# Attention in a one-core transformer kernel: 128-key score matmuls against four groups of 32 keys, with scores one step further ahead and the squares dealt out anew

## What is computed

```python
def _L0_attn_ref(x, w_qkv, w_proj, b_proj):      # x: (4, 1024, 256), H = 16 heads of 16
    qkv = jnp.einsum('btc,fc->btf', x, w_qkv)
    ...
    scores = jnp.einsum('bhqd,bhkd->bhqk', q, k) * hs ** (-0.5)
    p = jax.nn.softplus(scores)
    p = p * p
    p = p * jnp.tril(jnp.ones((t, t), dtype=p.dtype))
    attn = p / (jnp.sum(p, axis=-1, keepdims=True) + 1e-09)
    out = jnp.einsum('bhqk,bhkd->bhqd', attn, v)
```

## Time and profile before

| what | value |
|---|---|
| median of three runs | 1603.25 us (1602.64 to 1603.25) |
| the profiled execution | 1605.87 us |
| its span in the trace | 1604.0 us |
| attention phase in it | from 275.7 us to about 626 us |
| TensorE busy over the span | 1520.9 us (95%) |
| VectorE, ScalarE, GpSimd busy | 1216.4, 873.0, 411.4 us |
| DMA in the attention phase | about 100 GB/s |

### The profile page before, as it was taken

How to read it: one execution, slowest core, us unless ns; L and a number is a source line. 1 busy time by engine, 2 the same in 40 slices (tenths; PEclk the granted TensorE clock), 3 DMA queues, 4 the chain that set the end, 5 groups by cost and what they waited for, 6 DMA issues and landing times. The chain is left out here.

```text
span 1604.0 us, 28965 instructions
## 1 busy us (share of the span) xinstructions
PE 1520.9 (95%) x11188; PEld 1125.0 (70%) x11188; DVE 1216.4 (76%) x2334; ACT 873.0 (54%) x1372; POOL 411.4 (26%) x382
## 2 busy tenths in 40 slices
PE   8999898999999998999989999979999999899998
PEld 7888776444444446888867778756777777678777
DVE  4554797898999986664578888768777777688886
ACT  3333387988888886332332222278888887321220
POOL 0002111222122224100433221113555555211111
PEclk9999999999999999999999999999999999999999
DMA  4000065777777750000100000022333333100000
GB/s 159 26 1 14 20 188 178 100 95 106 106 101 102 100 72 2 14 1 1 40 27 8 1 1 1 1 69 78 102 101 107 106 107 107 40 14 27 14 27 27
DMA packets 57160, 95.83 MB, mean 60 GB/s; under 512 B 7904, under 2 KB 29632, under 8 KB 57024
## 3 DMA queue, kind: packets, MB, share of 16 engines
q1 hardware_dynamic: 56064, 93.38, 26.4%
q10 hardware_dynamic: 960, 0.59, 0.1%
HBM read 76.91 MB, written 17.04 MB: 59 GB/s over the span
## 5 line engine op out<-in xcount | busy, mean ns | idle before, releaser
L1438 DVE TENSOR_TENSOR att_weights<-att_weights 128x1024 f32<-128x1024 f32 (+1 forms) x224 | 267.7, 1241 | 39.4 <-ACT att_weights L1411 39.1
L928 DVE SCALAR_TENSOR_TENSOR X<-ps,moe_gsel,X 128x256 f32<-128x256 f32 x512 | 246.1, 483 | 63.5 <-PE ps L48 41.1
L1411 ACT ACTIVATE att_weights<-ps 128x1024 f32<-128x1024 f32 (+1 forms) x288 | 264.9, 992 | 39.8 <-PE ps L1347 20.5
L48 PE MATMUL ps<-w_experts_hi,moe_xh 128*128 128x512 f32 x512 | 205.1, 401 | 1.1 <-DVE X L928 1.1
L48 PE MATMUL ps<-w_experts_hi,moe_xl 128*128 128x512 f32 x512 | 203.3, 397 | 0.0
L48 PE MATMUL ps<-w_experts_lo,moe_xh 128*128 128x512 f32 x512 | 201.6, 394 | 0.0
L1367 PE MATMUL ps<-att_weights,att_v_ones 64*32 64x64 f32 (+5 forms) x2048 | 157.6, 400 | 0.0
L424 ACT ACTIVATE ffn_gates<-ps,ffn_gate_bias 128x512 f32<-128x512 f32 x72 | 49.5, 688 | 148.3 <-PE ps L48 126.6
L48 PEld LDWEIGHTS ps<-w_experts_hi,moe_xh 128*128 128x128 f32 x512 | 96.2, 188 | 27.9 <-DVE X L928 4.5
L48 PEld LDWEIGHTS ps<-w_experts_lo,moe_xh 128*128 128x128 f32 x512 | 96.1, 188 | 22.1
L48 PEld LDWEIGHTS ps<-w_experts_hi,moe_xl 128*128 128x128 f32 x512 | 96.3, 188 | 20.3
(11 more groups left out here) (281 smaller groups left out, 3672.1 us busy)
## 6 DMA issues: line engine op xcount, KB each, us to landing
ssm_lb<-decays SPq DMA_DIRECT2D x32, 512.0 KB, 4.7
ssm_rise<-decays SPq DMA_DIRECT2D x28, 512.0 KB, 3.9
qk_parts<-qkv_part SPq DMA_DIRECT2D x32, 384.0 KB, 2.8
q_stack<-qk_parts SPq DMA_DIRECT2D x64, 128.0 KB, 4.6
k_stack<-qk_parts SPq DMA_DIRECT2D x64, 128.0 KB, 7.8
att_q_stack<-qk_parts SPq DMA_DIRECT2D x64, 128.0 KB, 4.8
att_k_stack<-qk_parts SPq DMA_DIRECT2D x64, 128.0 KB, 8.8
out<-X SPq DMA_DIRECT2D x7, 512.0 KB, 2.9
```

The source lines that it names most:

```text
L48: ins = pe.matmul(out, l(k), r(k), start=first and n == 0, stop=last and n == len(passes) - 1)
L928: dve.scalar_tensor_tensor(out=x, in0=ring[:, e // 2, (e % 2) * C:(e % 2 + 1) * C], scalar=gsel[:, s, j, e:e + 1], in1=x, op0=ALU.mult, op ...
L1411: act.activation(Wt[:, u % WU, 0:n], scores(u)[:, 0:n], ACT.Softplus).then_inc(p_done, 1)
L1438: dve.tensor_tensor(wt, wt, wt, ALU.mult).then_inc(sq_done["dve"], 1)
```

## The change

The scores are computed by four matmuls with 32 keys each in place of one with 128 (`KG = 32`), each in its own column group; the masks too, and only for the groups that hold a masked key (two of four); the opening matmuls of UPPER units likewise become four over 128 rows. The matmul with zeros (L1358) goes, and the first REST tile opens the sum. The scores run five steps ahead of the values instead of four, and three of the four output stages stand one unit later. ScalarE squares the units 2, 7, 11 and 15 of a pass (before 6, 9 and 14), GpSimd none (before 11), VectorE 14 as before. What is computed stays the same.

```diff
--- before.py
+++ after.py
@@ -1278,11 +1278,12 @@
     step_units = [[u for u in range(NU) if step_of[u] == m] for m in range(NS)]
     BLOCK_STEPS = [m for m in range(NS) if m % PS == PS - 1 or pass_steps[m % PS + 1][0] != pass_steps[m % PS][0]]
     BLOCK_UNITS = [step_end[m] for m in BLOCK_STEPS]
-    STEPS_AHEAD = 4
-    TURN_LAG, COPY_LAG, DEN_LAG, OUT_LAG = 2, 7, 9, 10
+    STEPS_AHEAD = 5
+    TURN_LAG, COPY_LAG, DEN_LAG, OUT_LAG = 2, 8, 10, 11
     SU, WU = 3, 12
+    KG = 32
     assert NU % SU == 0 and NU % WU == 0
-    BY_ACT, BY_POOL = (6, 9, 14), (11,)
+    BY_ACT, BY_POOL = (2, 7, 11, 15), ()
     squarer = ["act" if u % PU in BY_ACT else "pool" if u % PU in BY_POOL else "dve" for u in range(NU)]
 
     def squares(by, i, u):
@@ -1333,18 +1334,21 @@
                 upper = segments[0][-1] == UPPER
                 pe.wait_ge(p_done, i * NU + u + 1)
                 if upper:
-                    low = slice(0, HALF)
                     pe.sem_inc(scores_free, 1)
-                    for r in range(2):
-                        pe.matmul(scores(u)[r * HALF:(r + 1) * HALF, 0].rearrange("p (s q) -> p s q", q=HALF), neg[low, low],
-                                  ident16[low, low].unsqueeze(1).broadcast_to([HALF, BANK // HALF, HALF]), start=True, stop=False)
+                    for g in range(P // KG):
+                        at = g * KG % HALF
+                        pe.matmul(scores(u)[g * KG:(g + 1) * KG, 0].rearrange("p (s q) -> p s q", q=HALF), neg[:, at:at + KG],
+                                  ident16[:, 0:HALF].unsqueeze(1).broadcast_to([P, BANK // HALF, HALF]), start=True, stop=False)
                 for n, (h, kj, t, c, q, w, part) in enumerate(segments):
-                    rows = slice(h % 2 * HALF, (h % 2 + 1) * HALF) if part == UPPER else slice(0, P)
-                    keys = slice(kj * P, kj * P + (HALF if part == UPPER else P))
-                    ins = pe.matmul(scores(u)[rows, t, c:c + w], SK[s][:, h, keys], SQ[s][:, h, q:q + w],
-                                    start=not upper, stop=n >= len(segments) - 2 if upper else part == FULL)
+                    groups = range(h % 2 * HALF, (h % 2 + 1) * HALF, KG) if part == UPPER else range(0, P, KG)
+                    for g in groups:
+                        keys = kj * P + (g % HALF if part == UPPER else g)
+                        masked = part == REST and g >= HALF
+                        ins = pe.matmul(scores(u)[g:g + KG, t, c:c + w], SK[s][:, h, keys:keys + KG], SQ[s][:, h, q:q + w],
+                                        start=not upper, stop=n >= len(segments) - 2 if upper else not masked)
                     if part == REST:
-                        ins = pe.matmul(scores(u)[:, t, c:c + HALF], neg[:, :], ident16[:, HALF:P], start=False, stop=True)
+                        for g in range(HALF, P, KG):
+                            ins = pe.matmul(scores(u)[g:g + KG, t, c:c + HALF], neg[:, g:g + KG], ident16[:, HALF:P], start=False, stop=True)
                 ins.then_inc(s_done, 1)
 
             def value_step(i, m):
@@ -1354,8 +1358,6 @@
                     pe.wait_ge(v_copied, 2 * (2 * i + s + 1))
                 if products[0][1] == 0 and not upper:
                     pe.wait_ge(o_done, (i * 2 + s) * BLOCKS + qb + 1)
-                    if qb == 0:
-                        pe.matmul(O(qb), ident16[:, :], neg[:, 0:1].broadcast_to([P, BANK]), start=True, stop=False)
                 for u in step_units[m]:
                     pe.wait_ge(sq_done[squarer[u]], squares(squarer[u], i, u))
                 if upper:
@@ -1365,7 +1367,7 @@
                     rows = slice(h % 2 * HALF, (h % 2 + 1) * HALF) if part == UPPER else slice(0, P)
                     values = va_up[rows, s, kj, h // 2] if part == UPPER and h % 2 else va[rows, s, kj, h]
                     ins = pe.matmul(O(qb)[h * 2 * HD:(h + 1) * 2 * HD, q0:q0 + w], values,
-                                    Wt[rows, (s * PU + unit) % WU, t, c:c + w], start=kj == 0 and part == FULL, stop=part == UPPER and kj == (qb + 1) * GT - 1)
+                                    Wt[rows, (s * PU + unit) % WU, t, c:c + w], start=kj == 0 and part != UPPER, stop=part == UPPER and kj == (qb + 1) * GT - 1)
                 ins.then_inc(pv_done, 1)
 
             def turn_output(n, i, k):
```

## The result

The changed kernel takes 1621.95 us in the median of 4 runs (1615.6 to 1628.21), the kernel before beside it 1602.95 us (1600.72 to 1603.25). The ratio is 1.0111, 95% interval 1.0086 to 1.0136: slower by 1.1%, 19 us, where 49 were forecast. The direction and the mechanism came as predicted; the forecast change is two and a half times too large, and the predicted 1652 us is wrong.

What follows compares the result with a forecast made beforehand. TensorE was taken to bound the attention's 21.3 us pass; afterwards 18.6 us of work, 5.3 idling for instructions and 0.5 slow clock make 24.4, 3.1 us x 16 = +49 us, so 1652 us in the median, range 1585 to 1700.

Steps and rivals of the forecast that it cites:

- What bounds the kernel before: Attention passes: TensorE is the bound, 20.5 us of work in a pass of 21.33, some 0.8 left for waiting.
- TensorE's own work after: Attention pass after the change: TensorE's steps sum to 18.6 us, with FULL scores 3.52, REST 4.48 and values 6.88.
- rival 4: Score steps: column groups overlap only twofold, +0.9 us on each of 8 large steps, pass 26 us, 1680 us; chance 0.03.
- rival 2: TensorE's score steps: changes of form stay or small weight loads replace them, pass near 20.5 us, 1590 us; chance 0.09.
- The number of packets: TensorE's instruction queue in the attention phase: 63 or so packets instead of 37, 3.9 a pass.
- Where the pauses lie: TensorE's issue idling: inside the stack loads, one or two pieces a pass, at distances of multiples of 256 instructions.
- How long they are: TensorE's idling for instruction packets queued behind stack loads: 5.3 us of every pass, from 2.7 to 7.9.
- the 640 instructions: TensorE's stock ten us into the loads: half a packet, one loaded and one more, lasting 13.2 us.
- The clock: TensorE's clock drops behind long gaps, worth up to 1.7 us of work; 0.5 us a pass taken.
- the forecast's own balance: Attention pass: 18.6 us plus idling equals the old 21.3 at 2.7 us of idling; below that, the change gains.
- rival 1: TensorE's instructions keep up with the column groups: a pass takes 19.4 us, median 1572 us; chance 0.18.
- Rival 3: TensorE's idling at its upper bound, 7.9 us, clock down after each: pass 27 to 28 us, about 1700; chance 0.10.

Runs made afterwards that it cites:

- groups_only_paced: Changed kernel with the steps ahead, lags and squares of the kernel before, its stack loads issued one at a time: 1585.55 us, ratio 0.9881.
- squares_only: Kernel before with only the new squares, four in a pass on ScalarE and none on GpSimd: 1607.25 us, ratio 1.0019.
- after_paced: Changed kernel with its 16 stack loads of a pass issued one by one along the next pass: 1580.51 us, ratio 0.9865.
- half_loads: Changed kernel without the key stacks' reloads in passes 3 to 16, query stacks still loaded at once: 1578.16 us, ratio 0.9834.
- after_noload: Changed kernel with the stack reloads of passes 3 to 16 left out: 1578.30 us, ratio 0.9849.
- paced_mix: Changed kernel with loads one at a time and unit 11's square given from ScalarE back to GpSimd: 1583.22 us, ratio 0.9864.

## Why the prediction was right and wrong

- **What bounds the kernel before**: right in the main. TensorE, with a pass of 21.27 us where 21.33 was read: less work on TensorE alone makes it 20.36 (groups_only_paced). But TensorE is not alone, as squares_only shows: a fourth square on ScalarE, which the forecast had well below the bound at 19.2 us, made the pass 21.86.
- **TensorE's own work after**: too low by 0.4 us. In a pass without pauses of after_paced, from start to start, FULL scores before values take 0.87, values 0.86 to 0.88 (0.97 in front of the transposes), UPPER values 0.58, transposes 0.59. The eight values come to 7.17 us where 6.88 were taken, but 0.24 for changes of form beside each set of transposes and 0.10 ahead of UPPER values had been counted there. REST scores are 4.47 in sum without a wait, as predicted (4.48). What was missed: the UPPER scores take 0.52 and 0.67 us, not 0.47, and FULL scores 3.87 in place of 3.52, one of them with 0.25 us more than the others and one with a change ahead of UPPER values. All in all 19.04 and 0.77 of waiting for ScalarE's softplus, 19.81. In its sum the forecast put that wait at nothing, so the base of 18.6 is 1.2 us too low. That the fourfold overlap of column groups holds was an estimate, and it does (0.87 us for 16 matmuls of 512 columns): rival 4 is out, and so is rival 2, a pass near 20.5 with little idling.
- **The number of packets**: right. 63 start in the phase (276.8 to 649.1 us), as forecast, and 37 did before.
- **Where the pauses lie**: right. Inside the loads or just behind them, at multiples of 256 instructions, one or two in most passes, with ScalarE and VectorE waiting for TensorE.
- **How long they are: this is the step that failed.** 5.3 us of every pass were forecast, and 2.6 measured (41.1 / 16), just under the lower bound of 2.7. The step is "During them the first packet of instructions starts some 10 us in and the next only as they end". The queues show three packets where it has two: at 1.0, 8.0 and 16.3 us after the first DMA of 437.25, and in the other passes mostly at -1 to 2, 4 to 10 and 13 to 17. The loads are issued over 7 to 10 us and have landed after 16 to 19, so the backlog grows while they are being issued. By the worked-out points, a packet that can be asked for at their start starts within one or two us; about 4 us in it waits 2.5 to 5, and 5 to 10 us in it waits 5 to 10. The prediction gave every packet the wait of the late ones, "6 to 8 us to the start". So TensorE has more in hand than the 640 instructions: behind 437.25 it ran dry after 16.0 us, not 13.2, and in nine of the ten pauses of over 2.3 us after 14 to 17. It went on after 19.3 us there, and after 16.7 to 19.3 in those nine, where 18.5 were forecast. Half a us of the 2.7 lies in the other term: from the start of a packet to its use 3.5 us were taken and 3.0 measured. With half of the DMAs, as in half_loads, the worst wait is 4.1 us and the pauses are nearly gone: the same rule, at another size.
- **The clock**: right, 0.5 us a pass. In the phase 30.7 us lie at half clock behind eight of the pauses. The phase is 48.8 us longer than in after_noload (372.3 against 323.5 us), and 41.1 of that are pauses: 7.7 us, 0.5 a pass, are left for the slow clock and all else. That is less than the half of 30.7 that slower work alone would cost; where the rest went was not measured.
- **The sum**: 18.6 + 5.3 + 0.5 = 24.4 forecast; 19.8 + 2.6 + 0.5 = 22.9 measured, against 23.0 read from the starts. That is 1.4 us too much a pass, 22 of the 27 us by which the profiled execution was missed. Five more lie in the kernel before, whose passes are 21.6 in the mean and not 21.3, with the four that have pauses (24.84 the longest). And the median of after lies 6.3 us under its profiled execution, where 2.6 were taken. Two errors work against each other here: the idling 2.7 us too high, the base 1.2 too low. That the miss is only 1.4 is luck, and so in part is the direction: by the forecast's own balance, 18.6 us plus the idling against 21.3, idling of 2.6 would have left the kernel no slower. It is slower because the base is 19.8; with that and the clock the balance lies near 1.3 us of idling (21.6 - 19.8 - 0.5).
- **The rivals**: rival 1, instructions in time, is what the kernel with loads one at a time shows, and its 1572 us would have been 1580. Rival 3, idling of 7.9 us, is out with the idling measured.

The windows of the changed kernel ahead of the end of the pause at 309.51, and behind it:

```profile
308.00:310.00 2.00, 0.49 (x28) 0.40 (x31) 0.07 (x1) 1.37 (x2) 0.00 (x0) 1.00 1.07 138
310.00:313.50 3.50, 3.50 (x37) 1.24 (x33) 3.05 (x3) 1.94 (x2) 1.93 (x2) 0.51 0.92 118
```

TensorE idles, and then the clock stands at half (1.2 GHz), with 37 matmuls in 3.5 us, as it did in the earlier trace rows.

The Trainium skill, which spoke against the stall in the prediction ("Runtime: NRT & Kernel Launch", Instruction fetch mechanics), calls the crossing of a 16 KB border mostly hidden and gives TensorE room for 2048 instructions. Here 25 crossings of 63 weren't hidden, 41.1 us in all. Of the stock, the pause before 456.57 decides: at 453.2 TensorE had used up a packet started at 445.2, with none started between. Another page of the Trainium skill, "Advanced Engine Details and Errata", ISA Cache, has 128 KB on TensorE and yet "Only 2 cache lines!" of 256 instructions. The second half of that agrees with the trace, by the same pause.

## What to carry to other kernels

Where a change multiplies small instructions, count them against the packets that bring them: the time of 256 instructions, here 5 us, against the wait of a packet behind the DMAs issued at once, with the 3 us or so from its start to its use. The remedy here was not fewer bytes or fewer instructions but a few lines on the queue that loads: the same 16 DMAs issued along the work that they have time for turned 1.1% slower into 1.4% faster. When a backlog is estimated, give each request the queue that stands when it comes, not the one at the end. And before a base is called the bound, count the waits that stay in it: here they and small slips in the work made 1.2 us a pass, nearly half of the error in the idling.

## What the runs showed of the hardware

- A packet of TensorE's instructions waits behind data DMAs issued before it: 9.7 us at most beside 16 DMAs of 128 KB issued at once, 4.1 beside 8, 3.9 beside 16 issued one at a time, 2.4 beside none. These are from worked-out points of asking.
- From the start of a packet to the end of the pause that waited for it passed 2.9 to 3.1 us in the ten longest pauses of the changed kernel, 3.7 in the longest of the kernel before.
- Eight of the ten pauses of 2.3 to 3.6 us were followed by 3.4 us at half clock (once 6.8), 30.7 us in all; the two that end at 523.66 and 595.10 were not.
- Four column groups of 32 with bf16 operands of 512 columns run side by side: 16 matmuls in 0.87 us, 0.22 for four. In float32 the same form takes 0.86 us for 8 records of 512 columns.
- A square of GpSimd slows the squares of VectorE beside it: 1343 ns each in paced_mix against 1215 in after_paced, which differ in that one square of a pass. In the kernel before, the 16 squares of VectorE that overlap one of GpSimd take 2172 ns, the others 1257.
